# Two-layer adaLN transformer on one core: attention masks in rounded 32-bit format, weighted values one unit later, gates through DRAM

## What is computed

```python
mod = (_silu(L0_c) @ L0_wmod).reshape(B, 6, 1, -1)
ga = (2 * (ga >= 0) - 1) * jnp.maximum(jnp.abs(ga), 0.25)      # gb likewise
h = _layernorm(x) * (1 + ca) + sa
x = x + ga * attention(h)        # 32 heads of 16, 8 key/value groups, causal, softmax
h = _layernorm(x) * (1 + cb) + sb
x = x + gb * experts(h)          # 64 experts of rank 8, the 16 best gated
```

## Time and profile before

| | us |
|---|---|
| Median of 3 runs | 963.16 (961.65 to 963.75) |
| The profiled execution | 961.87 |
| Its span on the core | 960.1 |
| TensorE busy | 878.6 (92%) |
| VectorE busy | 696.6 (73%) |
| ScalarE busy | 532.9 (56%) |
| GpSimd busy | 190.7 (20%) |
| Mean granted TensorE clock | 0.975 |

### The profile page before, as it was taken

The page is one execution under the profiler, slowest core; times in us unless marked ns, Lnnn a source line. Parts: engine busy times, 40 slices in busy tenths (PEclk is TensorE's granted clock), DMA queues, the critical chain, the costliest instruction groups (busy, mean ns, idle before and its releaser), DMA issues.

```text
span 960.1 us, 13802 instructions
## 1 busy us (share of the span) xinstructions
PE 878.6 (92%) x5224; PEld 673.5 (70%) x5224; DVE 696.6 (73%) x892; ACT 532.9 (56%) x707; POOL 190.7 (20%) x197
## 2 busy tenths in 40 slices
PE   3798879998989889898999999999988999999996
PEld 1556545655556668676888888688866888888885
DVE  3836757888898678768677778587787766767842
ACT  3313645566665344387666666576827766666830
POOL 3003534567556403300000000000040000000004
PEclk9798979999999999999999999999999999999999
DMA  9588676665535073173333333223336333342202
GB/s 314 172 232 150 48 67 114 107 109 100 73 66 166 21 34 93 50 45 110 109 99 98 99 100 97 80 88 93 106 51 81 108 91 93 106 109 67 67 1 88
DMA packets 41171, 93.57 MB, mean 97 GB/s; under 512 B 7057, under 2 KB 10129, under 8 KB 41105
## 3 DMA queue, kind: packets, MB, share of 16 engines
q1 hardware_dynamic: 36976, 87.33, 42.4%
q10 hardware_dynamic: 4128, 5.36, 1.6%
HBM read 75.89 MB, written 2.10 MB: 81 GB/s over the span
## 4 chain that ended last, share of the span: by engine, by line
PE 74%; DVE 11%; ACT 6%; issue 5%; SPq 2%; POOL 1%; ACTq 1%; DMA 0%; POOLq 0%; DVEq 0%
PE PS L1502 14%; PE PS L1504 13%; PE PS L1503 13%; PE PS L1807 5%; PE PS L1808 5%; PE PS L1806 5%; PE PS L1600 4%; PE PS L1632 3%; PE PS L1615 3%; DVE MX L1288 2%; ACT PT L872 2%; DVE ACC L1150 1%; PE PS L1524 1%; SPq L549 1%; ACT PL L832 1%
## 5 line engine op out<-in xcount | busy, mean ns | idle before, releaser
L832 ACT ACTIVATE PL<-CODE 128x1024 f32<-128x1024 int32 x200 | 201.7, 1056 | 58.4 <-DVE ACC L1150 55.5
L1502 PE MATMUL PS<-HH,WRH 128*128 128x512 f32 x448 | 176.0, 393 | 12.2 <-DVE HL L1109 5.1
L1504 PE MATMUL PS<-HL,WRH 128*128 128x512 f32 x448 | 175.1, 391 | 0.0
L1503 PE MATMUL PS<-HH,WRL 128*128 128x512 f32 x448 | 175.0, 391 | 0.0
L709 POOL TENSOR_TENSOR X<-X,SCR 128x512 f32<-128x512 f32 x32 | 42.5, 1341 | 561.1 <-DVE SCR L1135 561.0
L1150 DVE SCALAR_TENSOR_TENSOR ACC<-PL,ACC 128x1024 f32<-128x1024 f32 x100 | 124.0, 1240 | 8.7 <-DVE ACC L1150 0.5
L872 ACT ACTIVATE PT<-PS 128x512 f32<-128x512 f32 x160 | 85.4, 604 | 71.7 <-PE PS L1615 52.6
L1288 DVE TENSOR_REDUCE MX<-PS 128x2 f32<-128x256 f32 (+3 forms) x128 | 99.8, 818 | 29.2 <-PE PS L1602 15.8
L725 POOL TENSOR_TENSOR QS<-ident,MX 64x256 fp32r<-64x256 f32 x128 | 96.9, 757 | 77.0 <-DVE MX L1288 70.0
L1502 PEld LDWEIGHTS PS<-HH,WRH 128*128 128x128 f32 x448 | 84.5, 189 | 32.3 <-issue 7.3
L1600 PE MATMUL PS<-KS,QS 128*128 128x128 f32 (+3 forms) x256 | 86.5, 420 | 16.3 <-DVE MX L1288 13.5
(11 more groups left out here) (225 smaller groups left out, 1501.0 us busy)
## 6 DMA issues: line engine op xcount, KB each, us to landing
CODE<-in_CODES SPq DMA_DIRECT2D x50, 512.0 KB, 3.5
SCALE<-in_SCALES SPq DMA_DIRECT2D x100, 256.0 KB, 4.1
WM<-in_WM SPq DMA_DIRECT2D x12, 1024.0 KB, 5.4
QS<-FH SPq DMA_DIRECT2D x32, 128.0 KB, 4.1
QS<-FL SPq DMA_DIRECT2D x32, 128.0 KB, 5.3
X<-in_X ACTq DMA_DIRECT2D x2, 1024.0 KB, 12.1
GAB<-MR SPq DMA_DIRECT2D x8, 256.0 KB, 16.0
out_x<-X ACTq DMA_DIRECT2D x8, 256.0 KB, 2.0
```

The lines of the kernel that those rows point to most:

```text
L832: nc.scalar.activation(PL[:, n % 3], CODE[:, p % 2], ACT.Prelu, scale=scale, bias=bias, alpha=alpha).then_inc(s_plane, 1)
L1502: nc.tensor.matmul(dst, lh, rh, start=start and k == 0, stop=False)
L1503: nc.tensor.matmul(dst, ll, rh, start=False, stop=False)
L1504: ins = nc.tensor.matmul(dst, lh, rl, start=False, stop=stop and k == KC - 1)
```

## The change

- `identB` and `maskB` as operands of L1602 and L1618 become `identR` and `maskR`, both F32R. `identR` is now the middle third of padR; ScalarE fills `maskR` from `maskB` once before the attention, and the old copy into a tile of its own goes.
- The loop of TensorE issues `weighted` at odd n for units n - 5 and n - 4. `copy_even` goes from unit 4 of eight to unit 5, `copy_odd` from 2 to 4, the swap from 3 to 5, the inversions from 4 and 5 to 7 and 8, the division from 6 to 9 (in the last four units 5, 6 and 7). The decoding steps go from units 0, 1, 7 to 2, 4, 6, code pieces 3 to 5 load one or two groups later, and the rounding of pair 6 goes from unit 62 to 63.
- Behind the stack of group 3 SyncE stores the eight gate rows to a DRAM tensor in two DMAs. Each `spread_gates` is then one DMA from DRAM to all of GAB; the first is issued when the last transposed scores of the attention are done.

```diff
--- before.py
+++ after.py
@@ -69,7 +69,7 @@
 GU1, DN1 = 29, 43
 PIECES = 50
 
-PIECES_AT = {0: (0, 1), 5: (2,), 7: (3,), 10: (4,), 12: (5,)}
+PIECES_AT = {0: (0, 1), 5: (2,), 8: (3,), 11: (4,), 14: (5,)}
 STACKS = 3
 RING = 3
 LAG = 4
@@ -78,7 +78,7 @@
 
 LOW_RANK_AT = [(0, KC - 1), (1, 1), (1, KC - 1)]
 PAIRS = GROUPS // 2
-ROUND_AT = {41: 0, 46: 1, 49: 2, 54: 3, 58: 4, 60: 5, 62: 6}
+ROUND_AT = {41: 0, 46: 1, 49: 2, 54: 3, 58: 4, 60: 5, 63: 6}
 SPLIT_AT = {46: 0, 51: 1, 54: 2, 59: 3}
 SWAP = list(range(HD, 2 * HD)) + list(range(HD))
 
@@ -115,7 +115,7 @@
 
 def step_at(n):
 
-    slots = (0, 1, 7)
+    slots = (2, 4, 6)
     if not 0 <= n < B * GROUPS * TB or n % 8 not in slots:
         return None
     return divmod(n // 8 * len(slots) + slots.index(n % 8), STEPS)
@@ -123,7 +123,7 @@
 
 def pair_at(n, unit):
 
-    return n // 8 - 1 if n >= 8 and n % 8 == unit else None
+    return (n - unit) // 8 - 1 if n - unit >= 8 and (n - unit) % 8 == 0 else None
 
 
 PROJECTIONS = [key for b in range(B) for key in [("q", b, h) for h in range(REP)] + [("vt", b), ("k", b), ("v", b)]]
@@ -249,9 +249,10 @@
         GAB = sb("GAB", [P, B, D], F32)
         MCOL = sb("MCOL", [P, 2, 4, KC, B], F32)
         ident = sb("ident", [P, P], F32)
-        identR = sb("identR", [P, P], F32R)
+        maskR = sb("maskR", [P, P], F32R)
         identB = sb("identB", [P, P], BF16)
         padR = sb("padR", [P, 3 * P], F32R)
+        identR = padR[:, P:2 * P]
         maskB = sb("maskB", [P, P], BF16)
         sumsel = sb("sumsel", [P, 32], F32)
         CT = sb("CT", [P, 2, KC, B], F32)
@@ -357,6 +358,8 @@
 
         XN = [sb(f"XN{n}", [P, TB, D], F32, R0 + off * K) for n, off in enumerate((40, 40, 40, 40))]
         XM = [sb(f"XM{n}", [P, 2, D], F32, R0 + off * K) for n, off in enumerate((72, 16, 80, 48))]
+
+        GD = nc.dram_tensor("gates", (4, B, D), F32, kind="Internal").ap()
 
         PS = ctx.enter_context(nc.psum_tensor("PS", [P, 8, 512], F32))
 
@@ -428,6 +431,7 @@
         s_ph = sem("projection_weights_rounded")
         s_pl = sem("projection_weights_split")
         s_ll = sem("lora_weights_split")
+        s_gd = sem("gates_stored")
         s_gab = sem("gates_spread")
         s_sg = sem("silu_ready")
         s_hsh = sem("hidden_rounded")
@@ -525,13 +529,12 @@
         def spread_gates(sp, i):
 
             if i == 0:
-                sp.wait_ge(s_mr, 1)
                 sp.wait_ge(s_mm, J["modcol", 1, COLS[-1]] + 1)
+                sp.wait_ge(s_mx, 2 * B * GROUPS * TB)
             else:
                 sp.wait_ge(s_free, J[last_gated(i - 1)] + 1)
-            for b in range(B):
-                row = 64 * (i // 2) + 32 * (i % 2) + b
-                sp.dma_start(GAB[:, b], MR[row:row + 1].unsqueeze(1).to_broadcast([1, P, D])).then_inc(s_gab, 16)
+            sp.wait_ge(s_gd, 16 * B)
+            sp.dma_start(GAB[:], GD[i:i + 1].to_broadcast([P, B, D])).then_inc(s_gab, 16)
 
         def load_stack(sp, n):
 
@@ -620,7 +623,9 @@
             for n in range(B * GROUPS):
                 load_stack(sp, n)
                 if n == STACKS:
-                    spread_gates(sp, 0)
+                    sp.wait_ge(s_mr, 1)
+                    for b in range(B):
+                        sp.dma_start(GD[:, b], MR[b:P:32]).then_inc(s_gd, 16)
                 for p in PIECES_AT.get(n, ()):
                     load_piece(sp, p)
             sp.wait_ge(s_used, len(CAPS) * N_QKV)
@@ -630,6 +635,7 @@
             sp.wait_ge(s_wf, N_QKV - 1)
             sp.dma_start(ATF[:], a["AT"].rearrange("(c p) n -> p c n", p=P)).then_inc(s_at, 16)
             sp.wait_ge(s_st, STC(B * GROUPS))
+            spread_gates(sp, 0)
             sp.dma_start(LQF[:], a["LQKV"]).then_inc(s_lq, 16)
             sp.dma_start(LOAF[:], a["LO"][:, 0:KC * P]).then_inc(s_lo, 16)
             sp.dma_start(LOBF[:], a["LO"][:, KC * P:]).then_inc(s_lo, 16)
@@ -773,7 +779,6 @@
             act.wait_ge(s_sct, 1)
             nc.scalar.activation(SCT[:, :, :, 0:B], CT[:], ACT.Silu).then_inc(s_silu, 1)
             act.wait_ge(s_ident, 16)
-            nc.scalar.activation(identR[:], ident[:], ACT.Copy).then_inc(s_silu, 1)
             for i in range(3):
                 nc.scalar.activation(padR[:, i * P:(i + 1) * P], ident[:], ACT.Copy, scale=float(i == 1)).then_inc(s_silu, 1)
 
@@ -857,6 +862,8 @@
                 if step_at(n) and step_at(n)[1] < STEPS - 1:
                     curves(*step_at(n))
 
+            act.wait_ge(s_const, 16 * 3)
+            nc.scalar.activation(maskR[:], maskB[:], ACT.Copy).then_inc(s_silu, 1)
             act.wait_ge(s_free, J["gsum",] + 1)
             for n in range(3):
                 ride(n)
@@ -872,7 +879,7 @@
                     nc.scalar.activation(block_of(n, jc)[:].rearrange("p h i -> p (h i)"), PS[:, 4 + done % 3],
                                          ACT.Exp, scale=HD ** -0.5).then_inc(s_exp, 1)
                     done += 1
-                if n % 8 == 4:
+                if n % 8 == 5:
                     copy_even(act, n // TB - 1)
                 ride(n + 3)
                 if step_at(n) and step_at(n)[1] == STEPS - 1:
@@ -1129,7 +1136,7 @@
                 t = key[-1]
                 dve.wait_ge(s_mm, J[key] + 1)
                 if t == 0:
-                    dve.wait_ge(s_gab, 16 * B * ({"wo": 0, "y": 1, "down": 2 + key[1]}[key[0]] + 1))
+                    dve.wait_ge(s_gab, 16 * ({"wo": 0, "y": 1, "down": 2 + key[1]}[key[0]] + 1))
                 if added(key) > 2:
                     dve.wait_ge(s_xadd, added(key) - 2)
                 nc.vector.tensor_tensor(SCR[:, t % 2], PS[:, bank(key)], GAB[:, t // TB], ALU.mult).then_inc(s_free, 1)
@@ -1291,15 +1298,15 @@
                     curve_sum(*step_at(n))
                 if n == TB - 1:
                     gate_values()
-                if pair_at(n, 2) is not None:
-                    copy_odd(pair_at(n, 2))
-                if pair_at(n, 3) is not None:
-                    swap_sums(pair_at(n, 3))
-                for half in range(2):
-                    if pair_at(n, 4 + half) is not None:
+                if pair_at(n, 4) is not None:
+                    copy_odd(pair_at(n, 4))
+                if pair_at(n, 5) is not None:
+                    swap_sums(pair_at(n, 5))
+                for half, unit in enumerate((5, 6) if n >= 60 else (7, 8)):
+                    if pair_at(n, unit) is not None:
                         invert(half)
-                if pair_at(n, 6) is not None:
-                    divide(pair_at(n, 6))
+                if pair_at(n, 7 if n >= 60 else 9) is not None:
+                    divide(pair_at(n, 7 if n >= 60 else 9))
                 if n in SPLIT_AT:
                     split_heads(SPLIT_AT[n])
 
@@ -1586,7 +1593,7 @@
 
             units = B * GROUPS * TB
             pe.wait_ge(s_free, J["gsum",] + 1)
-            pe.wait_ge(s_silu, 2)
+            pe.wait_ge(s_silu, 5)
             blocks = [0, 0]
 
             def scores(n):
@@ -1599,7 +1606,7 @@
                     for h in (2 * half, 2 * half + 1):
                         nc.tensor.matmul(PS[:, h, 0:(ic + 1) * P], QS[:, q % STACKS, h, ic * P:(ic + 1) * P],
                                          KS[:, q % STACKS, 0:(ic + 1) * P], start=True, stop=True)
-                        ins = nc.tensor.matmul(PS[:, h, ic * P:(ic + 1) * P], identB[:], maskB[:], start=False, stop=True,
+                        ins = nc.tensor.matmul(PS[:, h, ic * P:(ic + 1) * P], identR, maskR[:], start=False, stop=True,
                                                skip_group_check=True)
                     ins.then_inc(s_s, 1)
 
@@ -1615,7 +1622,7 @@
                     ins = nc.tensor.matmul(dst, KN[q % STACKS][:, jc * P:(jc + 1) * P],
                                            QS[:, q % STACKS, :, ic * P:(ic + 1) * P], start=True, stop=jc < ic)
                     if jc == ic:
-                        ins = nc.tensor.matmul(dst, maskB[:], identB[:].unsqueeze(1).to_broadcast([P, REP, P]),
+                        ins = nc.tensor.matmul(dst, maskR[:], identR.unsqueeze(1).to_broadcast([P, REP, P]),
                                                start=False, stop=True)
                     ins.then_inc(s_st, 1)
                     blocks[0] += 1
@@ -1634,13 +1641,13 @@
                                                start=(jc == 0), stop=(jc == ic), tile_position=(0, 32 * h))
                 ins.then_inc(s_pv, 1)
 
-            for n in range(units + 3):
+            for n in range(units + 4):
                 if n < units:
                     scores(n)
                 if 2 <= n < units + 2:
                     transposed(n - 2)
-                if n >= 3 and n % 2 == 0:
-                    for unit in (n - 4, n - 3):
+                if n >= 5 and n % 2 == 1:
+                    for unit in (n - 5, n - 4):
                         weighted(unit)
             pe.wait_ge(s_mx, 2 * units)
             pe.wait_ge(s_exp, blocks[0])
@@ -1714,7 +1721,7 @@
```

(2 more changed lines are left out.)

## The result

The changed kernel takes **952.35 us** (median of 4 runs, 949.76 to 953.1) against 962.78 for the kernel before (4 runs): a ratio of 0.9887, 95% interval [0.9865, 0.9909], about 11 us. That lies in the range on record, 938 to 955, but 7 above the forecast of 945.4 and on the 952.4 of rival B, in which only the gates bring something. The profiled execution of the changed kernel took 952.0 us, with a span of 950.1.

The account below looks back on a forecast made before the run. TensorE and VectorE, nearly full and feeding each other, were taken to bound the attention, with a SyncE queue stall at the gates. Gates -10.8 and regrouping -7.0 sum to -17.8: 945.4 us on the median's scale, range 938 to 955.

Parts of the forecast that it names:

- rival B: Attention: VectorE's wait moves to TensorE, waiting for bank 7 or exponentials; only the gates gain: 952.4 us, chance 0.23.
- Gates: SyncE's queue around group 5: spreading gates from DRAM removes the slow copies' blocking; saves 10.8 us, bounds 9 and 12.
- Masks: TensorE's score and transposed-score masks in rounded 32-bit format: 0 us, within 1 over all 64 units.
- Rival A: TensorE's mask weight loads not covered: 320 x 0.108 = 34.6 us added, 980 us; chance 0.04.
- Regrouping: Attention: weighted values one unit later remove VectorE's seven 1.0 us waits before copying odd groups; 7.0 us saved.
- VectorE goes straight on to unit 5's maxima, whose scores are there, so nothing should reach the path: Unit 5 of eight: TensorE may wait 0.5 us for bank 7's copy, at no cost; otherwise 4 us come back.
- I take 7.0: Gain from weighted values one unit later: 7.0 us, between -4 given back and 12.
- The moved decoding, sums and divisions ... I take 0: Attention: same instructions in other units; 0 us, within 1 either way.
- The last codes land about a unit before ScalarE wants them: 0, at worst 1.: SyncE's queue: code pieces load one or two groups later yet arrive in time; cost 0, at worst 1 us.
- The heaviest unit of VectorE becomes the last of eight ... even.: Last unit of eight: maxima and an inversion beside TensorE's 56 products, where a curve sum stood; no net change.
- What would show it: Trace signs, including a beat near 11.9 us per group and VectorE the fuller engine; forecast wrong if it stays 12.3.

Follow-up runs that it names:

- e8: Kernel before, with the gates stored to DRAM and spread from there, but at the old place behind group 3's stack: 951.28 us, ratio 0.9892.
- e10: e5 with the old 16-bit masks: 945.65 us, ratio 0.9833.
- e4: Changed kernel with the codes of piece 5 loaded behind group 13 instead of 14: 949.42 us, ratio 0.9869.
- e5: e4 with GpSimd's scaling and adding of a piece each one unit later: 946.90 us, ratio 0.9840.
- e9: Changed kernel with the decoding steps back in units 0, 1, 7 and the code pieces at their old groups: 958.14 us, ratio 0.9960.
- e1: Kernel before with only the gates' part: stored to DRAM and spread from there at the later place: 953.12 us, ratio 0.9897.
- e11: e5 with ScalarE's rounding of the output weights (WOH) one unit earlier: 944.45 us, ratio 0.9821.
- e7: Kernel before, still spreading the gates from MR in SBUF, but first issued behind the last transposed scores: 958.75 us, ratio 0.9968.

## Why the prediction was right, and where it was wrong

**Gates: right.** Forecast 10.8, bounds 9 to 12; alone they gave 9.9 (10.9 in the stretch of the table). No 15 us issue, a landing of 3.8 us inside the 4 to 6, no wait of VectorE for GAB. The reasons on record, that the queue's issue was the culprit and that scale loads spread over 128 partitions from DRAM land in 4.1, hold: e8 shows it. The place is worth 3.1 by itself, since what was saved at 114 us was mostly paid at 307.

**Masks: right.** 0 within 1 was forecast, 1.2 alone and nothing in e10 measured. Rival A falls: 320 loads grew by some 99 ns each, and only the masks of 128 columns show any of it in the chain, 0.11 for 0.07, as the forecast had them; the wider ones are 0.01 shorter. What the prediction had not weighed is that the 16-bit loads stood idle for 21.7 us, time that the longer ones mostly fill.

**Regrouping: the step that failed** is "VectorE goes straight on to unit 5's maxima, whose scores are there, so nothing should reach the path", with "I take 7.0" on it, and "The moved decoding, sums and divisions ... I take 0". The wait went, as said. But the prediction looked for what comes next only at TensorE and bank 7, one unit behind. It came from two other queues.

- *SyncE.* "The last codes land about a unit before ScalarE wants them: 0, at worst 1." ScalarE waited 2.1 us for them, and the clock fell in the ten us after. The prediction had the rule in hand (a stack occupies the queue for 10 of 12.3 us) and took a margin from it without setting the codes' place behind stack 14 against the unit of their first use. Undone in e4: 952.35 to 949.42, and 4.1 us in the stretch of the table (216.2 to 212.1). But 1.3 of these lie in units 0 to 31, before the edit can act; 2.2 are at the end, where it does.
- *GpSimd.* The prediction moved VectorE's and ScalarE's steps and did not follow the piece on to GpSimd, whose scaling stands in a fixed order among the diagonals. Undone in e5: 2.5 to 3.1 us.
- *VectorE's own load.* "The heaviest unit of VectorE becomes the last of eight ... even." It is not even: an inversion is 1.74 us, the curve sum that stood there 1.24. Over units 24 to 55 the median period of the last unit of eight rose from 3.40 to 4.04 us, that of unit 4, which got the copies, from 2.45 to 3.36, and that of unit 2 fell from 4.26 to 2.87. No run shows what this costs alone; e9 shows that the old slots and the old code groups beside the later values cost 7 us.

**The size came out by luck in part.** With both queues mended, e5 is 6.2 us under e1 by the medians and 5.6 in the stretch, where 7.0 was forecast; 946.9 stands where the prediction had 945.4. But only 2.8 of the 5.6 is idle time of VectorE, the thing that the 7.0 was read from. The rest is busy time, chiefly the last division, 0.69 us instead of 3.41 because GpSimd's subtraction no longer runs beside it (last section), which no term of the sum had. Rival B came true in its number, though not by its mechanism: it had TensorE waiting "as long for bank 7 or for exponentials", and it was the diagonals, the codes and the end.

**"What would show it"** had given the sign: B if the beat stays. Over units 32 to 55 it is 12.7 us a group before and in e1 and 12.9 after; only in e5 is it shorter, 12.3, by the 0.4 that the prediction wanted (12.3 to 11.9 on its stretch). VectorE did not become the fuller engine, and in e5 it still is not (66.3 us against 69.3 for TensorE in these units).

**Open.** What VectorE's maxima wait for in the 5.9 us of "issue" is not visible. That the clock's fall from 255 us on comes from the late codes rests on e4, which changes both together. Whether a piece 5 earlier still, or its scaling in yet another unit, gives more was not tried, nor was the order of the last fold, WOH and exponentials in any other way than e11's.

## What to carry to other kernels

When a step is moved, follow its data through every engine and every queue to the last reader, and at each one write down two times, when it comes and when it is wanted; an in-order queue that issues one step too early holds up what stands behind it. A wait that can be pointed at gives a price for a change, but whether it has been earned is read from the whole stretch, with idle and busy time of the nearly full engine side by side: seven waits of 1.0 us went here, and VectorE's idle time rose by 4.5 us while its busy time fell by 3.0. A row that many partitions need should not be read many times from one partition while anything else uses the queue.

## What the runs showed of the hardware

**The slow copy holds up whatever is behind it.** In e7 it is no longer a stack but two plain loads from DRAM that take 6.74 and 9.60 us to issue; the same loads issue in 0.44 and 0.43 in the changed kernel:

```profile
289.50 0.44 SPq L639 DMA_DIRECT2D LQF<-in_LQKV  x1
289.98 0.43 SPq L640 DMA_DIRECT2D LOAF<-in_LO  x1
```

**VectorE and GpSimd side by side.** The last division of the attention took 3.43 us before and 0.70 after, with the same form. Before, GpSimd's subtraction for ATL ran beside it; after, it had started earlier, beside the inversions, and was done. Before, VectorE and then GpSimd:

```profile
306.42 3.43 DVE L1225 TENSOR_TENSOR NUM<-NUM,DENS 128x512 f32<-128x512 f32 x1
```

```profile
304.70 4.61 POOL L742 TENSOR_TENSOR ATL<-ATF,ATH 128x2048 fp32r<-128x2048 f32 x1
```

After:

```profile
300.08 0.70 DVE L1232 TENSOR_TENSOR NUM<-NUM,DENS 128x512 f32<-128x512 f32 x1
```

```profile
295.61 4.62 POOL L748 TENSOR_TENSOR ATL<-ATF,ATH 128x2048 fp32r<-128x2048 f32 x1 [2.40 <-ACT ATH L894]
```

GpSimd's subtraction ends at 309.31 before (304.70 + 4.61), and the division, begun at 306.42, ends at 309.85, half a microsecond later. The two inversions beside it, one input each, took the usual 3.54 for two after. The Trainium skill (SBUF — State Buffer, Who interferes with whom) says that a VectorE instruction with two SBUF inputs contends with a GpSimd instruction that reads SBUF; the trace agrees, and puts 2.7 us on it. In e1 the division takes 3.41 as well, and in both kernels the first output tile follows right behind it, so this shortens the end. Part of it is lost again on the way there: the low parts of the output weights (WOL) and of three heads (FL), also made from two inputs each, take 2.96 and 4.03 us after where they took 2.29 and 2.99 in e1. From the start of WOL to the first tile it is 13.4 us after and 14.4 in e1.
